# A gated graph network step: z gate accumulated onto the r sum in PSUM, first layer's products in the freed banks

## The reference

```python
x = layernorm(x + (adj @ x) @ weight + bias)
h = x
for _ in range(3):
    a  = adj @ h                      # a_in and a_out are the same product here
    av = concat([a, a])
    z  = sigmoid(av @ w3.T + b3 + h @ u3.T + bu3)
    r  = sigmoid(av @ w4.T + b4 + h @ u3.T + bu3)
    hv = tanh(av @ w5.T + b5 + (r * h) @ u5.T + bu5)
    h  = (1 - z) * h + z * hv
out = layernorm(x + h)
```

## Time and profile before

| what | value |
|---|---|
| median of 3 runs | 1685.92 us (1685.49 to 1685.96) |
| span of the profiled execution, first to last instruction | 1681.9 us |
| TensorE matmuls busy | 1644.3 us, 98% of the span |
| VectorE busy | 1479.1 us, 88% |
| ScalarE busy | 919.9 us, 55% |
| GpSimd busy | 167.9 us, 10% |
| mean granted TensorE clock | 0.994 of full speed |
| DMA | 166.48 MB, mean 99 GB/s |

### The profile page before, as it was taken

One profiled execution on the slowest core, in us unless ns is written; L12 is line 12 of the kernel. 1 busy time (PEld: TensorE's weight loads), 2 busy tenths in 40 slices (PEclk: granted clock), 3 DMA queues, 4 the chain that ended last, 5 costly groups with the idle time before them and its releaser, 6 DMA issues.

```text
span 1681.9 us, 24763 instructions
## 1 busy us (share of the span) xinstructions
PE 1644.3 (98%) x8608; PEld 1412.0 (84%) x8608; DVE 1479.1 (88%) x2312; ACT 919.9 (55%) x1286; POOL 167.9 (10%) x168
## 2 busy tenths in 40 slices
PE   6999999999999999999999999999999999999997
PEld 5888888888888888888888888888888888888885
DVE  5789898998888989899898989989899888898987
ACT  3555555565555556555555555555556555555663
POOL 3001001010010101001010010100101001010001
PEclk8999999999999999999999999999999999999998
DMA  3123233232422423224332342323323242243321
GB/s 111 51 75 126 76 100 112 87 125 81 128 82 82 131 91 121 93 75 133 104 112 75 100 125 87 125 75 106 106 87 125 85 127 81 81 131 100 101 82 63
DMA packets 172021, 166.48 MB, mean 99 GB/s; under 512 B 16352, under 2 KB 147936, under 8 KB 172000
## 3 DMA queue, kind: packets, MB, share of 16 engines
q1 hardware_dynamic: 172000, 166.20, 31.0%
HBM read 84.35 MB, written 81.79 MB: 99 GB/s over the span
## 4 chain that ended last, share of the span: by engine, by line
PE 92%; DVE 4%; ACT 2%; issue 1%; DMA 0%; POOL 0%; SPq 0%; DVEq 0%; ACTq 0%
PE ps_r L308 30%; PE ps_h L308 29%; PE ps_z L308 15%; PE ps_x L318 13%; PE ps_x L351 5%; DVE hv L683 1%; DVE hv L679 1%; DVE a_lo_b L582 1%; DMA x_in_b<-x 0%; ACT z_sb L563 0%; ACT h_hi_b L467 0%; DVE rh L767 0%; ACT rh L542 0%; ACT hv L503 0%; PE ps_z L318 0%
## 5 line engine op out<-in xcount | busy, mean ns | idle before, releaser
L542 ACT ACTIVATE rh<-ps_r,bias_r 128x512 f32<-128x512 f32 x192 | 132.2, 689 | 211.4 <-PE ps_r L308 211.4
L467 ACT ACTIVATE u_sb<-ps_r 128x1024 f32<-128x1024 f32 x96 | 98.8, 1030 | 195.2 <-PE ps_r L308 195.2
L683 DVE TENSOR_TENSOR hv<-hv,z_sb 128x512 f32<-128x512 f32 x192 | 149.5, 779 | 6.6
L503 ACT ACTIVATE hv<-ps_h,bias_h 128x512 f32<-128x512 f32 x192 | 130.7, 681 | 35.4 <-PE ps_h L308 35.4
L582 DVE TENSOR_TENSOR rh_lo<-rh,rh_hi 128x512 fp32r<-128x512 f32 x192 | 132.3, 689 | 9.5
L467 ACT ACTIVATE rh_hi<-rh 128x512 fp32r<-128x512 f32 x192 | 120.5, 628 | 23.1 <-DVE rh L767 23.1
L318 PEld LDWEIGHTS ps_x<-adjt,h_nat 128*128 128x128 f32 x1024 | 123.9, 191 | 5.4 <-ACT h_nat L467 0.6
L308 PE MATMUL ps_h<-rh_hi,u_hi 128*128 128x512 f32 x384 | 127.1, 412 | 0.0
L563 ACT ACTIVATE z_sb<-z_sb,bias_z 128x512 f32<-128x512 f32 x192 | 126.9, 709 | 0.0
L755 DVE TENSOR_TENSOR z_sb<-ps_z,u_sb 128x1024 f32<-128x1024 f32 x96 | 116.6, 1214 | 11.3 <-PE ps_z L308 11.3
L318 PE MATMUL ps_x<-adjt,h_nat 128*128 128x128 f32 x1024 | 124.7, 275 | 0.0
(11 more groups left out here) (152 smaller groups left out, 4193.1 us busy)
## 6 DMA issues: line engine op xcount, KB each, us to landing
h_scratch<-h_blocks SPq DMA_DIRECT2D x128, 256.0 KB, 2.0
h_moved_in<-h_scratch SPq DMA_DIRECT2D x512, 64.0 KB, 2.0
h_scratch<-h_blocks SPq DMA_DIRECT2D x30, 512.0 KB, 2.6
x_in_a<-x SPq DMA_DIRECT2D x16, 512.0 KB, 4.5
x_in_b<-x SPq DMA_DIRECT2D x16, 512.0 KB, 5.6
out<-result_a SPq DMA_DIRECT2D x16, 512.0 KB, 3.0
h_moved_in_a<-h_scratch SPq DMA_DIRECT2D x60, 128.0 KB, 3.4
h_moved_in_b<-h_scratch SPq DMA_DIRECT2D x60, 128.0 KB, 3.0
```

Of the source, the lines that this page charges most:

```text
L467: return act.activation(dst, src, ACT.Copy)
L503: act.activation(hv[:, c, :], ps_h[:, c, :], ACT.Tanh, bias=bias_h[:, c:c + 1]).then_inc(hv_ready, 1)
L542: r = act.activation(rh[:, c, :], ps_r[:, c, :], ACT.Sigmoid, bias=bias_r[:, c:c + 1])
L683: dve.tensor_tensor(hv[:, c, :], hv[:, c, :], z_sb[:, c, :], ALU.mult).then_inc(scaled_ready, 1)
```

## The change

z's sum is h @ u3 + a @ w3 and r's is h @ u3 + a @ w4, so z's is r's plus a @ (w3 - w4). The changed kernel subtracts the summed w4 from the summed w3 once, and accumulates a with that difference onto ps_r after ACT has read r's sum from it. ACT reads z's sum from ps_r directly. u_sb, its copy and the addition on DVE are gone. ps_z is then free in the loop, and takes the next pair's first-layer products, which stood in ps_x. TensorE's order in a slot becomes u3, first layer, w4, w5, w3 (chunk by chunk, each behind r_ready), u5.

```diff
@@ tensor: slot
                 if not begin:
-                    pe.wait_ge(r_ready, 2 * i)
+                    pe.wait_ge(z_ready, i)
-                split_product(ps_r, "u3", h_hi[g], h_lo[g], True, True, u_done)
+                split_product(ps_r, "u3", h_hi[g], h_lo[g], True, False)
...
+                if not last and k in (1, 3):
+                    if not (isinstance(p, int) and p == 0 and k == 1):
+                        pe.wait_ge(y_added, group_no(p + 1, k // 2))
+                    first_graph(ps_z, p + 1, k // 2)
+                if not last and k in (2, 4):
+                    first_weights(ps_z, ax_hi, ax_lo, p + 1, k // 2 - 1)
...
-                if not begin:
-                    pe.wait_ge(z_added, i)
-                split_product(ps_z, "w3", a_hi[g], a_lo[g], True, True, z_done, a_parts)
-                if not last and k in (1, 3):
-                    first_graph(ps_x, p + 1, k // 2)
-                if not last and k in (2, 4):
-                    first_weights(ps_x, ax_hi, ax_lo, p + 1, k // 2 - 1)
-                pe.wait_ge(u_copied, i + 1)
-                split_product(ps_r, "w4", a_hi[g], a_lo[g], False, True, r_done)
+                split_product(ps_r, "w4", a_hi[g], a_lo[g], False, True, r_done, a_parts)
...
                 split_product(ps_h, "w5", a_hi[g], a_lo[g], True, False)
+                for o in range(C):
+                    pe.wait_ge(r_ready, 2 * i + o + 1)
+                    split_product(ps_r, "w3", a_hi[g], a_lo[g], False, True, z_done, None, range(o, o + 1))
...
                     pe.wait_ge(h_nat_ready, 2 * (move_no(p, k - 1) + 1))
-                    if not last and k in (1, 3):
-                        pe.wait_ge(ax_lo_ready, group_no(p + 1, k // 2) + 1)
-                    elif not last:
-                        pe.wait_ge(y_added, group_no(p + 1, k // 2 - 1) + 1)
@@ scalar
-            act.wait_ge(gate_sum, 3)
-            for n, name in enumerate(("u3", "w3", "w4", "w5", "u5")):
+            act.wait_ge(gate_sum, 4)
+            for n, name in enumerate(("u3", "w4", "w5", "w3", "u5")):
...
-                act.wait_ge(u_done, 2 * i + 2)
-                copy(u_sb[:, :, :], ps_r[:, :, :]).then_inc(u_copied, 1)
...
-                    first_graph_parts(ps_x, ax_hi, p + 1, k // 2)
+                    first_graph_parts(ps_z, ax_hi, p + 1, k // 2)
...
-                act.wait_ge(z_added, i + 1)
+                if not begin:
+                    act.wait_ge(scaled_ready, 2 * i)
                 for c in range(C):
-                    z = act.activation(z_sb[:, c, :], z_sb[:, c, :], ACT.Sigmoid, bias=bias_z[:, c:c + 1])
+                    act.wait_ge(z_done, 2 * i + c + 1)
+                    z = act.activation(z_sb[:, c, :], ps_r[:, c, :], ACT.Sigmoid, bias=bias_z[:, c:c + 1])
@@ vector
+            dve.wait_ge(gate_sum, 2)
+            dve.tensor_tensor(w_raw[0][:, 0:C, :], w_raw[0][:, 0:C, :], w_raw[1][:, 0:C, :],
+                              ALU.subtract).then_inc(gate_sum, 1)
...
-                dve.wait_ge(u_copied, i + 1)
-                dve.wait_ge(z_done, 2 * i + 2)
-                dve.tensor_tensor(z_sb[:, :, :], ps_z[:, :, :], u_sb[:, :, :], ALU.add).then_inc(z_added, 1)
...
-                    first_graph_parts(ps_x, ax_hi, ax_lo, p + 1, k // 2)
+                    first_graph_parts(ps_z, ax_hi, ax_lo, p + 1, k // 2)
-                    first_sum(ps_x, p + 1, k // 2 - 1)
+                    first_sum(ps_z, p + 1, k // 2 - 1)
```

More of the change, by code:

```diff
@@ L105, in gnn_kernel @@
         ax_hi, ax_lo = sb("ax_hi", [P, C, COLS], F32R), sb("ax_lo", [P, C, COLS], F32R)
-        u_sb = sb("u_sb", [P, C, COLS])
         z_sb = sb("z_sb", [P, C, COLS])
@@ L149, in gnn_kernel @@
         norm_constants = sem("norm_constants")
-        u_done, z_done, r_done, h_done = sem("u_done"), sem("z_done"), sem("r_done"), sem("h_done")
+        z_done, r_done, h_done = sem("z_done"), sem("r_done"), sem("h_done")
         graph_done = sem("graph_done")
@@ L154, in gnn_kernel @@
         ax_done, y_done = sem("ax_done"), sem("y_done")
-        u_copied, z_ready, r_ready = sem("u_copied"), sem("z_ready"), sem("r_ready")
+        z_ready, r_ready = sem("z_ready"), sem("r_ready")
         rh_hi_ready, hv_ready, h_hi_ready = sem("rh_hi_ready"), sem("hv_ready"), sem("h_hi_ready")
@@ L159, in gnn_kernel @@
         h_nat_ready, h0_t_ready = sem("h_nat_ready"), sem("h0_t_ready")
-        z_added, rh_ready, rh_lo_ready = sem("z_added"), sem("rh_ready"), sem("rh_lo_ready")
+        rh_ready, rh_lo_ready = sem("rh_ready"), sem("rh_lo_ready")
         diff_ready, scaled_ready = sem("diff_ready"), sem("scaled_ready")
@@ L393, in a_parts @@
                         pe.wait_ge(a_lo_ready, i + 1)
-                if not begin:
-                    pe.wait_ge(z_added, i)
                 if begin:
                     pe.wait_ge(gates_ready, 2)
-                split_product(ps_z, "w3", a_hi[g], a_lo[g], True, True, z_done, a_parts)
-                if not last and k in (1, 3):
-                    first_graph(ps_x, p + 1, k // 2)
-                if not last and k in (2, 4):
-                    first_weights(ps_x, ax_hi, ax_lo, p + 1, k // 2 - 1)
-                pe.wait_ge(u_copied, i + 1)
-                if begin:
-                    pe.wait_ge(gates_ready, 3)
-                split_product(ps_r, "w4", a_hi[g], a_lo[g], False, True, r_done)
+                split_product(ps_r, "w4", a_hi[g], a_lo[g], False, True, r_done, a_parts)
                 if last and k == SLOTS - 1:
@@ L421, in slot @@
                 if begin:
+                    pe.wait_ge(gates_ready, 3)
+                split_product(ps_h, "w5", a_hi[g], a_lo[g], True, False)
+                if begin:
                     pe.wait_ge(gates_ready, 4)
-                split_product(ps_h, "w5", a_hi[g], a_lo[g], True, False)
+                for o in range(C):
+                    pe.wait_ge(r_ready, 2 * i + o + 1)
+                    split_product(ps_r, "w3", a_hi[g], a_lo[g], False, True, z_done, None, range(o, o + 1))
                 def rh_parts(n, c):
@@ L730, in _ @@
             first_state_parts(0, 0, 0)
-            gate_low_part(1, "w3")
+            gate_low_part(1, "w4")
             graph_parts(0, 0)
-            gate_low_part(2, "w4")
+            gate_low_part(2, "w5")
             first_norm(0, 1)
-            gate_low_part(3, "w5")
+            gate_low_part(3, "w3")
             gate_low_part(4, "u5")
```

## The result

The changed kernel took 1672.35 us (median of 4 runs, 1670.4 to 1673.72) beside 1685.7 of the kernel before (1682.02 to 1685.96): ratio 0.9926, 95% interval 0.9908 to 0.9944. In a second comparison, of 8 runs against 13, it was 1674.11 against 1682.44, ratio 0.9952 (0.9936 to 0.9967).

What follows compares the result with a forecast made beforehand. TensorE, 98% busy, was taken as the bound, waiting only for a_lo_b in seven slots. Span 1681.9 - 11.0 (a_lo) + 1.2 (r_ready) + 0.6 (head) = 1672.7, plus 4.0 to the median: 1676.7 us, range 1674 to 1683.

Steps and rivals of the forecast that it cites:

- What bounds it: Whole loop: TensorE 98% busy, waiting only in seven slots for a_lo_b, when POOL's bias additions block DVE's state update.
- -11.0 us for a_lo: Slot 1, TensorE: first-layer products ahead of w4 cover the late a_lo_b, removing seven waits of 1.57 us, 11.0 together.
- r_ready 1.2 us: Slot 1, TensorE at w3: new waits until ACT has read r's sum, 1.2 us in all, bounds 0 and 5.0.
- POOL's shift of 1.7 us: Slot 5 into slot 0: earlier r sum and transpose of h0 let POOL's bias additions start 1.7 us earlier, bounds 0 and 2.7.
- Head +0.6: Before the loop: one more 128x512 subtraction on DVE delays the first norm and all behind it, +0.6 us, bounds 0 and 0.8.
- Tail 0: After the last slot: h_t_a's transposes come one product earlier without a wait, 0 us, bounds -0.1 and +0.5.
- The last line of the sum: From span to time: the three runs' median lay 4.0 us above the profiled span; kept, 1672.7 gives 1676.7 us.
- A: Slot 0: a transfer or SP holds x_in_a, so POOL keeps its old phase; waits cost 5.0, time 1680.5 us; chance 0.17.
- B: Slot 0: POOL starts too early and blocks rh_lo on DVE, delaying u5; 1695.5 us; chance 0.07 for both forms.
- its mild form: Slots 0 and 5: ACT's first-state copies hold r past w5, 31 slots losing 0.5 us each, 1691; chance within 0.07.
- C: The seven waits go, but small waits at w3 of about 0.5 us in 16 pairs cost 8 us: 1684.7; chance 0.07.

Runs made afterwards that it cites:

- before_split: The kernel before, with POOL's second bias addition waiting until slot 0's state is complete: 1668.5 us, ratio 0.9915 to the kernel before.
- before_pool_writes: The kernel before, with POOL's bias additions replaced by a tiny operation and write-only fills (x and bias don't reach the first sum): 1665.3 us, ratio 0.9883.
- after_pool_at_hv: The changed kernel, with POOL's two bias additions waiting for hv's first half in slot 0, so they start with DVE's update: 1682.6 us, ratio 0.9985.

## Why the prediction was right or wrong

**What bounds it: right.** TensorE dense but for slot 1, POOL's reads blocking DVE's two-input operations, POOL's hour set by the chain from slot 5: all held. before_split and before_pool_writes remove it by two different ways and give the same loop.

**-11.0 us for a_lo: mis-sized, and credited to the wrong part.** The slots' lengths show 13.1; I took the waits view for the whole loss. I also wrote that the wait goes "even if nothing else moves". It does, but after_pool_at_hv shows what comes in its place with POOL at its old hour: 1.2 us a pair for r and h_nat, where I had put 0.7 for r alone.

**r_ready 1.2 us: the wrong wait.** The excess of 3.1 us came at the graph product for h_nat. The long pairs of the kernel before had the same late transfer, hidden behind the wait for a_lo_b. ACT and TensorE in slot 1 of its first loop pair, which starts at 154.07:

```profile
168.17 1.14 ACT L467 ACTIVATE h_nat<-h_moved_in 128x512 f32<-128x512 f32 x2
```

```profile
170.07 1.95 PE L318 MATMUL ps_x<-adjt,h_nat 128*128 128x128 f32 x16
```

In the seven long pairs h_nat was complete 15.1 to 15.3 us into slot 1. In a short pair the graph product takes it at 14.0; in the long ones it came only at 15.9 to 16.0. I asked what follows a late second half of the state on ACT (h_hi, r) and left out its other reader, the transfer. The two errors cancel, by luck: the sum had -9.8 for the loop, the traces -9.7.

**POOL's shift of 1.7 us: right**, 1.9 measured, of which 0.5 is DVE's freed time.

**Head +0.6: right for the step, wrong for the whole.** The fourth subtraction shows in the trace after:

```profile
17.64 1.86 DVE L709 TENSOR_TENSOR w_raw<-w_raw 128x512 f32<-128x512 f32 x3
19.43 0.68 DVE L711 TENSOR_TENSOR w_raw<-w_raw 128x512 f32<-128x512 f32 x1
...
20.24 1.37 DVE L601 TENSOR_SCALAR h_nat_a<-h_nat_a,h_meanvar,h_rstd_sb 128x256 f32<-128x256 f32 x4
```

From the end of bn_aggr to the norm is 2.5 us where it was 2.1: +0.4. But all of it came 2.6 us earlier than in the earlier trace rows, because x_in_b landed 1.3 us earlier and its graph product took 2.5 us instead of 3.8. In twelve traces this point of the head lies anywhere between 17.1 and 20.0 us. I had taken one trace's head for fixed.

**Tail 0: within its bound**, +0.5; two traces of the unchanged kernel before differ by 0.3.

**The last line of the sum is the step that failed.** I put 4.0 us between the profiled span and the median. Every later run has its own span beside its time, and the difference is 1.8 to 2.3 us in each. The profiled execution was thus some 2 us faster than the median of the three runs shown (its own time isn't known), and 1672.7 + 1.8 = 1674.5 would have been the figure. With 1.8 in place of 4.0 the whole range would have been 1671.8 to 1680.8, and 1672.35 lies in it. The 2.2 us that are left between 1674.5 and 1672.35 are of the size of the head's scatter. With before scattering from 1676.2 to 1689.9 (number of long pairs, head), a range with a floor of 1674 around one trace and three runs was too narrow below.

**Rivals.** A (POOL doesn't move) is out: SP's issue moved by 1.9 us. B didn't occur; its mild form neither, slots 0 and 5 are at 15.4 throughout. C, small waits eating the gain, is what happened in kind, 3.1 us of it, though at h_nat and not at w3, and only in pairs with a late POOL.

## What to carry to other kernels

When a wait of the busiest engine comes only in some rounds of a loop, compare the good rounds with the bad before changing the work: here it was the start of an unrelated operation on POOL, and one semaphore wait (14.0 us) was worth more than a change that took away 215 us of elementwise work (8.3 us beside the same runs). Follow every reader of a late result, the transfers too, since a wait that goes uncovers the next one behind it. And take a slot's length in good and bad rounds as the price of a wait, since the list of waits leaves out what a restart costs.

## What the runs showed of the hardware

A DVE operation with two inputs in SBUF took up to 2.9 us instead of 0.69 beside a POOL addition of 2.4 us, and less where the addition was already under way (1.90 us in the first loop pair after). When both kept issuing they alternated, one instruction each: POOL's second addition took 2.85 us when DVE had got in between and 2.39 when it ran alone (before_split). One blocked operation ahead of a_lo_b did no harm in any pair of the two traces of the kernel before; two did in every pair. Operations with an input in PSUM (a_lo_b, 1.2 us) kept their time, and so did those with two inputs in SBUF beside POOL fills (0.64 to 0.72 us).
